# Image 1's pipeline fill rearranged: TensorE transposes, GpSimd adds of squares, cluster sums in one piece

## What is computed

```python
xn = x / jnp.maximum(jnp.linalg.norm(x, axis=1, keepdims=True), EPS)
cn = centroids / jnp.maximum(jnp.linalg.norm(centroids, axis=1, keepdims=True), EPS)
sim = jnp.einsum('bchw,nc->bnhw', xn, cn)
idx = jnp.argmax(sim, axis=1)
onehot = jax.nn.one_hot(idx, N, dtype=x.dtype)
sum_x = jnp.einsum('bhwn,bchw->bnc', onehot, x)
count = jnp.sum(onehot, axis=(1, 2))
centroids_local = sum_x / jnp.maximum(count, 1.0)[..., None]
gathered = centroids_local[jnp.arange(B)[:, None, None], idx]
delta = jnp.transpose(gathered, (0, 3, 1, 2)) - x
alpha = jnp.exp(-jnp.mean(delta * delta, axis=1, keepdims=True))
y = x + alpha * delta
out = jnp.einsum('oc,bchw->bohw', W, y) + b[None, :, None, None]
return jax.nn.relu(out)
```

## Time and profile before

| | us |
|---|---|
| median of 3 runs (414.55 to 415.38) | 415.17 |
| the profiled execution | 415.32 |
| its span in the trace | 413.5 |
| PE busy in the span | 407.3 |
| VectorE, ScalarE, GpSimd busy | 335.2, 255.3, 257.8 |
| first gather matmul of unit 3 / second | 63.68 / 67.30 |

### The profile page before, as it was taken

How to read it: one execution, slowest core, us unless ns; L and a number is a source line. 1 busy time by engine, 2 the same in 40 slices (tenths; PEclk the granted TensorE clock), 3 DMA queues, 4 the chain that set the end, 5 groups by cost and what they waited for, 6 DMA issues and landing times.

```text
span 413.5 us, 5729 instructions
## 1 busy us (share of the span) xinstructions
PE 407.3 (98%) x2064; PEld 287.4 (69%) x2064; DVE 335.2 (81%) x411; ACT 255.3 (62%) x352; POOL 257.8 (62%) x113
## 2 busy tenths in 40 slices
PE   8999999999999999999999999999999999999996
PEld 6744456775877767775867757776777758777885
DVE  2449979789789889899798898898798997898730
ACT  6565564766764775665855666756856657576541
POOL 2000564993699766993979936996769938424420
PEclk9999999999999999999999999999999999999999
DMA  7998496997689395966979575893967240222223
GB/s 261 318 281 160 84 245 171 299 255 150 212 213 297 102 244 161 275 173 170 270 168 250 195 157 190 245 264 115 250 165 220 103 137 3 103 101 103 101 78 126
DMA packets 82047, 76.69 MB, mean 185 GB/s; under 512 B 13844, under 2 KB 56852, under 8 KB 82020
## 3 DMA queue, kind: packets, MB, share of 16 engines
q1 hardware_dynamic: 82020, 76.33, 67.9%
HBM read 48.40 MB, written 25.17 MB: 178 GB/s over the span
## 4 chain that ended last, share of the span: by engine, by line
PE 91%; SPq 5%; DMA 3%; issue 1%; DVE 0%; ACT 0%; DVEq 0%
PE main L922 21%; PE main L923 21%; PE main L924 21%; PE fa L821 8%; PE sump L864 8%; PE gat L898 5%; DMA x<-x 3%; SPq L248 2%; SPq L264 1%; PE al L904 1%; PE fa L830 1%; PE main L966 1%; SPq L242 1%; PE gat L910 1%; PE al L910 1%
## 5 line engine op out<-in xcount | busy, mean ns | idle before, releaser
L922 PE MATMUL main<-yh,wh 128*128 128x512 f32 x376 | 153.5, 408 | 0.0
L923 PE MATMUL main<-yl,wh 128*128 128x512 f32 x376 | 146.7, 390 | 0.0
L924 PE MATMUL main<-yh,wl 128*128 128x512 f32 x376 | 146.6, 390 | 0.0
L331 POOL TENSOR_TENSOR z<-z,x 128x1024 f32<-128x1024 f32 x42 | 99.9, 2399 | 65.1 <-DVE z L458 65.1
L338 POOL TENSOR_TENSOR yl<-z,yh 128x1024 fp32r<-128x1024 f32 x44 | 105.7, 2421 | 54.9 <-ACT yh L616 54.9
L624 ACT ACTIVATE o<-main,bcol 128x512 f32<-128x512 f32 x96 | 65.5, 683 | 59.3 <-PE main L924 59.1
L922 PEld LDWEIGHTS main<-yh,wh 128*128 128x128 f32 x376 | 70.6, 188 | 22.0 <-issue 4.9
L924 PEld LDWEIGHTS main<-yh,wl 128*128 128x128 f32 x376 | 70.6, 188 | 15.2
L923 PEld LDWEIGHTS main<-yl,wh 128*128 128x128 f32 x376 | 70.7, 188 | 13.9
L345 POOL TENSOR_TENSOR xr<-xt 128x2048 f32<-128x2048 f32 x11 | 51.5, 4679 | 18.2 <-DVE xt L371 18.2
L434 DVE TENSOR_TENSOR z<-gat,x 128x1024 f32<-128x1024 f32 x46 | 56.0, 1217 | 6.4 <-PE gat L898 6.1
(11 more groups left out here) (121 smaller groups left out, 367.0 us busy)
## 6 DMA issues: line engine op xcount, KB each, us to landing
out<-o SPq DMA_DIRECT2D x23, 1024.0 KB, 7.3
x<-x SPq DMA_DIRECT2D x21, 1024.0 KB, 6.4
xs<-x SPq DMA_DIRECT2D x84, 256.0 KB, 5.5
x<-x SPq DMA_DIRECT2D x12, 256.0 KB, 5.7
o<-w SPq DMA_DIRECT2D x1, 1024.0 KB, 8.8
out<-o SPq DMA_DIRECT2D x4, 256.0 KB, 2.0
sq<-centroids SPq DMA_DIRECT2D x2, 80.0 KB
oht<-oh SPq DMA_TRANSPOSE x7, 3.7
```

What stands on the lines that cost most here:

```text
L331: pool.tensor_tensor(z, z, X[g // PARTS % 2][:, pair(h), span(g)], ALU.add).then_inc(y_pool, 1)
L922: t_.matmul(main[:, o % 2, :], WH[:, k, rows], YH[g % 2][:, k, :], start=(k == 0), stop=False)
L923: t_.matmul(main[:, o % 2, :], WH[:, k, rows], YL[g % 2][:, k, :], start=False, stop=False)
L924: last = t_.matmul(main[:, o % 2, :], WL[:, k, rows], YH[g % 2][:, k, :], start=False, stop=(k == KC - 1))
```

## The change

Five things are edited, all in the fill.

1. Units 4 and 5 of image 1 (TURNED) are no longer loaded in blocks and transposed by DVE. PE transposes them from X by 32 matmuls against the identity in four groups (`turn`), into the banks `gat` and `main`, and ACT evicts each group (`keep_turned`). Their tokens then lie in plain order (`plain(g)`). `load_xs(4)` and `(5)` go.
2. DIRECT = 3: units 0, 1 and 2 have their four channel blocks of squares added on POOL (`add_chunks`, three 128 x 512 additions a unit) and then summed by one full float32 ones matmul instead of four. Unit 2's squares go to `XR[:, 0]`.
3. The three `sum_clusters(1, .)` stand in one row on PE, in the order 1, 2, 0, and close ahead of the convolution of unit 0.
4. On DVE the argmax of image 1 stands ahead of unit 1's deltas. Unit 3's first transposed half stands ahead of the argmax, its second behind unit 1's deltas. The transposes of unit 6 move ahead of the loop. `y_half(1, 1)` and `low_half(1, 1)` go from POOL to DVE.
5. On SP the x loads of image 1 come first, then `load_xs(3)`, `(6)` and `(7)`, then `transpose_onehot(1)`, then x of units 6 and 7.

Core of the diff:

```diff
-DIRECT = 2
+DIRECT = 3
+
+TURNED = (PARTS + 1, PARTS + 2)
 def y_on_vector(g, h):
-    return g == 0 or (g >= TAIL and h == 1)
+    return g == 0 or (g == 1 or g >= TAIL) and h == 1
 def low_on_vector(g, h):
-    return g >= TAIL and h == 1
+    return (g == 1 or g >= TAIL) and h == 1
+def by_vector(g):
+    return sum(i not in TURNED for i in range(PARTS, g + 1))
+def blocks_loaded(g):
+    return sum(i not in TURNED and (g - i) % 2 == 0 for i in range(PARTS, g + 1))
             def load_xs(g):
-                wait(sp, tr_done, g - 2 - 2)
+                if blocks_loaded(g) > 1:
+                    wait(sp, tr_done, by_vector(g - 2))
...
             load_x(3)
-            load_xs(3)
             load_x(4)
             load_x(5)
-
-            sp.wait_ge(cop_done, 1)
-            load_xs(4)
-            load_xs(5)
+            load_xs(3)
+            load_xs(6)
+            load_xs(7)
             transpose_onehot(1)
-            load_xs(6)
             load_x(6)
-            load_xs(7)
             load_x(7)
             load_xs(8)
...
+            def add_chunks(g):
+                for h in range(2):
+                    sq = squares(g, h)
+                    pool.wait_ge(sq_done, 2 * g + h + 1)
+                    pool.tensor_tensor(sq[:, 0, :], sq[:, 0, :], sq[:, 1, :], ALU.add).then_inc(two_done, 1)
+                pool.wait_ge(two_done, 2 * g + 2)
+                first_two, last_two = squares(g, 0)[:, 0, :], squares(g, 1)[:, 0, :]
+                pool.tensor_tensor(first_two, first_two, last_two, ALU.add).then_inc(four_done, 1)
+
+            add_chunks(0)
+            add_chunks(1)
...
             def sum_squares_direct(g):
-                for k in range(KC):
-                    if k % 2 == 0:
-                        pe.wait_ge(sq_done, 2 * g + k // 2 + 1)
-                    last = t_.matmul(alpha(g), ones[:, :].bitcast(F32), OUT[g][:, k, :],
-                                     start=(k == 0), stop=(k == KC - 1))
-                last.then_inc(one_done, 1)
+                pe.wait_ge(four_done, g + 1)
+                t_.matmul(alpha(g), ones[:, :].bitcast(F32), squares(g, 0)[:, 0, :], start=True, stop=True
+                          ).then_inc(one_done, 1)
...
+            def turn(g, half):
+
+                if g == TURNED[0]:
+                    pe.wait_ge(z_done, 1 + half)
+                else:
+                    pe.wait_ge(xe_act, 6 + half)
+                for t in range(HALF):
+                    at = g % PARTS * UNIT + (HALF * half + t) * P
+                    for k in range(KC):
+                        last = t_.transpose((gat, main)[half][:, t, k * P:(k + 1) * P], X[1][:, k, at:at + P],
+                                            ident[:, :])
                 last.then_inc(xp_done, 1)
```

More of the change, by code:

```diff
@@ L195, in pair, with alpha @@
             return slice(2 * h, 2 * h + 2)
+        def alpha(g):
+            return gat[:, 0, :] if g == 1 else al[:, :]
         def banks(g, h):
-            return main if g < DIRECT and h == 1 else gat
+            return main if g < LAG and h == 1 else gat
         def squares(g, h):
             if g < DIRECT:
-                return OUT[g][:, pair(h), :]
+                return (OUT[0][:, :, :], OUT[1][:, :, :], XR[:, 0, :, :])[g][:, pair(h), :]
             return SQ[:, :, :] if h == 0 else gat[:, :, :]
@@ L353, in _ @@
                 low_half(g, 1)
+                if g == 1:
+                    add_chunks(2)
                 if g + 5 < UNITS and split(g + 5):
@@ L511, in _ @@
             low_weights(3)
[L513 to L517, removed]
+            delta(0, 0)
+            delta(0, 1)
+            transpose_half(3, 0)
             best_sims(1)
             first_best(1)
+            delta(1, 0)
+            delta(1, 1)
+            transpose_half(3, 1)
             scale(0, 0)
@@ L523, in _ @@
             y_half(0, 1)
-            transpose_half(4, 0)
-            transpose_half(4, 1)
+            low_clusters(1)
             scale(1, 0)
             scale(1, 1)
-            transpose_half(5, 0)
-            transpose_half(5, 1)
+            counts(1)
+            y_half(1, 1)
             delta(2, 0)
             delta(2, 1)
-            low_clusters(1)
-            counts(1)
-            add_squares(2)
             rest_of_mean(1)
             parts_of_mean(1)
-            fold(2)
-            low_sum(2)
+            transpose_half(6, 0)
+            low_half(1, 1)
+            transpose_half(6, 1)
             for g in range(PARTS, UNITS):
@@ L588, in keep_transposed, with keep_turned @@
                               ACT.Copy).then_inc(xe_act, 1)
+            def keep_turned(g, half):
+                done = PARTS * 2 + 2 * TURNED.index(g) + half + 1
+                act.wait_ge(xp_done, done)
+                a_.activation(XT[:, g % PARTS, HALF * half:HALF * (half + 1), :], (gat, main)[half][:, :, :],
+                              ACT.Copy).then_inc(xe_act, 1)
             def square(g, h):
                 act.wait_ge(z_done, 2 * g + h + 1)
-                if g < DIRECT:
+                if g < LAG:
                     act.wait_ge(wT_ps, KC)
@@ L631, in copy_sims @@
                 dst, src = simS[:, u, :, :].rearrange("p t s -> p (t s)"), simP[u]
-                if not plain(b):
+                if not plain(g):
                     dst = simS[:, u, :, :].rearrange("p t (q i) -> p q t i", q=Q)
@@ L717, in _ @@
             square(0, 1)
+            keep_turned(4, 0)
+            keep_turned(4, 1)
+            keep_turned(5, 0)
+            keep_turned(5, 1)
+            exp(0)
             square(1, 0)
             square(1, 1)
-            exp(0)
             copy_onehot(1)
+            high_half(0, 0)
+            copy_sums(1)
             exp(1)
-            high_half(0, 0)
             high_half(0, 1)
             count_onehot(1)
-            high_half(1, 0)
+            scale_means(1)
+            high_means(1)
             relu(0, 0)
@@ L737, in _ @@
             relu(0, 3)
-            high_sum(2)
             for g in range(PARTS, UNITS):
@@ L994, in _ @@
             similarities(5)
+            turn(4, 0)
+            transpose_sims(1)
+            turn(4, 1)
+            turn(5, 0)
+            turn(5, 1)
             gather(1, 0)
+            sum_squares_direct(0)
             gather(1, 1)
-            transpose_sims(1)
-            sum_squares_direct(0)
+            sum_clusters(1, 1)
+            sum_clusters(1, 2)
+            sum_clusters(1, 0)
             sum_squares_direct(1)
-            sum_clusters(1, 0)
+            pe.wait_ge(z_done, 4)
             pe.wait_ge(hi_done, 1)
@@ L1004, in _ @@
             high_passes(range(2, KC))
-            sum_clusters(1, 1)
+            gather(2, 0)
+            add_halves(1)
             wait_low(pe, 0, 0)
@@ L1012, in _ @@
                 last.then_inc(main_done, 1)
-            gather(2, 0)
-            sum_clusters(1, 2)
             gather(2, 1)
-            convolve(0, 2, range(0, 2))
-            add_halves(1)
-            convolve(0, 2, range(2, KC))
+            convolve(0, 2)
             convolve(0, 3)
```

45 lines of the change are left out of this document (21 added, 24 removed).

## The result

The changed kernel takes 416.72 us in the median of 5 runs (416.04 to 417.57), the kernel before 415.30 (5 runs, 414.55 to 415.38). The ratio is 1.0039 with a 95% interval of 1.0023 to 1.0056: slower by 0.4%, or 1.4 us. The forecast was 416.3, from 413.3 to 417.3, slower as the likeliest. The profiled execution, 416.04 us, is the fastest of the five; its span is 414.3 us and 0.8 over that of before.

A forecast was written before the change was run, and what follows sets the result against it. PE bounds the kernel, busy 407.3 of 413.5 us, so a shift of unit 3's second gather moves the end. One-hot landing plus 4.4 gives 58.3, plus 10.2 gives 68.5, +1.2: 416.3 us, range 413.3 to 417.3.

The forecast's parts named there:

- The DMA queue: On SP's queue: the transposing one-hot DMA, issued at 46.4, waits behind load_xs(7) and lands at 53.9, not 50.2.
- L: Moment the one-hot's transposing DMA lands: 53.0 to 54.4, taken as 53.9 us.
- rival 2: Same chain, but landing by most DMA engines only, 52.6 to 53.4: 415.0 to 415.8, no change; chance 0.25.
- main case: One-hot waits behind xs7 and lands from 53.4 to 54.6: 415.8 to 417.1 us; chance 0.45.
- The wait at the second gather of unit 2: PE, ready at 55.35, stalls 3 us for VectorE's delta(2,0), done L + 4.4 = 58.3.
- the mark: Start of unit 3's second gather on PE, 67.30 us before; forecast 10.2 after 58.3, at 68.5, +1.2.
- PE's own work: PE in the fill: ones matmuls -4.6, transposes +3.7, stalls -0.4 and -0.8, sum -2.1 us; about -1.7 after ScalarE waits.
- signs of being wrong: One-hot landing within 4.5 us, PE waiting for GpSimd at a ones matmul, clock under 1.00 near 40 us, idle PE after 68.
- rival 3: GpSimd's 128x512 add costs a whole 2.76 us, holding PE 2 us at the ones matmul: 418.3; chance 0.07.
- half price: GpSimd's 128x512 adds cost half its 128x1024 operations, 1.2 to 1.4 us each; 0 to +1.5 kept for it.
- Rival 1: One-hot does not wait for xs7, lands at 50.2; unit 3's second gather at 65.5, time 413.4; chance 0.2.
- Rival 4: PE clock falls to 1.2 GHz behind the four turns, up to 6 us more work, time 419; chance 0.03.

The follow-up runs named there:

- kernel with twice the traffic ahead: Changed kernel with x of unit 6 also issued ahead of transpose_onehot(1) on SP; 420.64 us, ratio to before 1.0119.
- one-hot-first kernel: Changed kernel with transpose_onehot(1) issued ahead of load_xs(7) on SP; 414.42 us, ratio to before 0.9982.

## Why the prediction was right, step by step

- **The bound.** Right: PE is busy 312.00 of 312 us from 68 to 380, and what was lost ahead stays lost.
- **The DMA queue.** Right, the step on which the sign hung. L was put at 53.9 and came at 52.95. As it stands that is in rival 2's bracket, 52.6 to 53.4, and not in the main case's from 53.4 on. Of the 0.9, 0.5 is that this execution ran earlier (unit 0's first gather at 31.70 instead of 32.28, so that the DMA was issued at 45.86, not 46.4). The rest would fit a landing nearer the average DMA engine's time than the slowest's, as rival 2 has it; that is not shown. With nothing, half a megabyte, one, and one and x ahead it landed at 48.6, 50.2, 52.95 and 55.5. Where the Trainium skill, DMA: Bandwidth & Descriptors, Queues, rings and completion order, has each DMA engine take its descriptors in ring order, these runs agree, a transposing DMA included (its packets began at 53 us behind those of x, above), which no row of before showed.
- **The wait at the second gather of unit 2.** 3.0 forecast, 2.49 measured. From L to the gather I summed 4.4 us, and it was 5.1. The term that was mis-sized is `y_half(1, 1)`: 1.14 by starts forecast from the operation of unit 0, 1.84 by starts measured (1.92 long). It began at 54.83 while GpSimd was at `y_half(1, 0)`, which the change had put into the same microseconds, and ended 1.1 us behind that one's end at 55.67. Where it met none of GpSimd's work, in the kernel with twice the traffic ahead, it took 1.21.
- **From there to the mark.** 10.2 forecast, 58.03 to 68.30 is 10.27.
- **PE's own work.** Right for the four turns in the 0.93 each, the ones matmuls at 0.86, the wait for unit 5's x that is gone (32.91 directly behind the gather), and that of the means matmuls. Wrong on one: I had unit 1's additions end before PE needs them. They ended at 47.45 against 46.77, PE waited 0.73, and that cost nothing, since PE then stood 2.49 us for the one-hot. A wait for GpSimd at a ones matmul was among my signs of being wrong, there for rival 3; it came, by another cause. PE was ready for the gather at 55.54, as against 55.35: the early execution and this wait cancel.
- **GpSimd's additions.** The half price was right where GpSimd was alone (1.27 to 1.28), and rival 3's 2.76 is out. It was wrong where VectorE had an operation on two SBUF operands at the same time: 2.15 for the third addition of unit 1, 3.54 for a pair of unit 2. I could have read this in the trace of before. The pair of the earlier trace rows, 2.76 each, began at 46.09 while VectorE was at unit 0's y until 46.98. And the 4679 ns of the earlier trace rows, from which I took that time goes with the columns, is a mean of such cases and others: that operation takes 3.60 us at 305.25, alone, one and a half times the 2.4 of one half as wide, and 5.95 at 318.23, where it meets VectorE's `xr<-xr`. The half price held, but these rows did not support it.
- **Rival 1**'s case, no wait behind xs7, is what the one-hot-first kernel made: 414.4, not 413.4. The 1.0 between is about the two waits for GpSimd, 0.7 and 0.6, that I had taken as hidden. With one of them edited away it is 413.7.
- **Rival 4**, the clock behind the transposes, did not come: 1.00 from 33 to 68 us with all four turns in it. The Trainium skill, TensorE: Matmul & The Clock Gate, Part 4: PE-mode transpose, would not count them as PE busy; this trace shows no fall behind them.
- **The number.** 416.3 forecast, 416.72 measured, and near by luck in part: L came 0.95 early and the chain behind it was 0.7 too long, and the two nearly cancel. From the prologue on, the mark moved by 1.6 us in the traces and the time by 1.4 in the medians, where I had 1.2. Of the 0.7 us by which the median lies over the profiled execution, some 0.6 is likely that execution's early prologue, which the 415.32 that I started from did not have. The range of 4 us held both signs, so that the time lies in it says little; it lies in the main case's narrower one, 415.7 to 417.2, too.

## What to carry to other kernels

Do not issue a DMA whose result a row of short operations waits for behind a large load that is needed only 20 us later; in these runs the order of issues on the one queue was the order of service, so count what is still in flight ahead of the small one. When a chain of small steps (here one-hot, counts, delta) shares in-order engines with the work on the critical path, look at what stands behind each of its waits on every engine: freeing VectorE alone only handed the wait to ScalarE. A gain in the bound engine's own work shows only up to the next thing that is late, so test each part of a change with the others' waits out of the way. And before reading a few tenths out of one trace, count from a point ahead of the change: here the prologue alone moved by over 1 us from one execution to the next.

## What the runs showed of the hardware beyond that

- An operation of VectorE on two float32 operands from SBUF and one of GpSimd did not run beside each other: in each of the meetings read from these traces, whichever began second stood until the first was through, and then took a little less than its usual time. Here are GpSimd and VectorE in the changed kernel:

```profile
45.30 2.15 POOL L368 TENSOR_TENSOR o<-o 128x512 f32<-128x512 f32 x1
47.48 5.85 POOL L350 TENSOR_TENSOR yl<-z,yh 128x1024 fp32r<-128x1024 f32 x2
53.29 2.38 POOL L343 TENSOR_TENSOR z<-z,x 128x1024 f32<-128x1024 f32 x1
```

```profile
45.02 1.28 DVE L491 TENSOR_TENSOR z<-z,x 128x1024 f32<-128x1024 f32 x1
47.47 1.23 DVE L491 TENSOR_TENSOR z<-z,x 128x1024 f32<-128x1024 f32 x1
```

  VectorE's first runs to 46.30, and GpSimd's addition, begun at 45.30, ends 1.15 us later, at 47.45; alone it takes 1.27. VectorE's second runs to 48.70, and GpSimd's pair, begun at 47.48, ends 4.63 us later, at 53.33; alone a pair takes 4.8. The other way round, VectorE's `y_half(1, 1)` took 1.92, 2.44 and 2.75 us in three kernels, and each time ended 1.1 us behind the GpSimd operation that it had met (55.67, 52.95 and 54.16). VectorE's operations with an operand in PSUM, as `scale` at 49.28 (2.35 for two, as ever), ran beside GpSimd without a loss. The Trainium skill, GPSIMD Engine Reference, section Specifications, says that GpSimd shares its SBUF interfaces with VectorE and contends with its instructions that have two SBUF inputs; the trace agrees, and shows the price as the rest of the other's instruction. So an operation moved from GpSimd to VectorE to make room, as `y_half(1, 1)` here, gives part of that back where the two engines then meet.
- The issue of a transposing DMA itself took 1.53 to 1.55 us on SP with nothing ahead of it in the queue, 2.08 behind half a megabyte, and 3.65 behind a whole one in 512-byte packets, but 2.44 behind the end of one and a megabyte of x; so it also holds what SP has to issue next.
- Behind a wait of PE of 5.2 us the next 5.9 us of its work took 1.1 us more, with the granted clock at its lower level for some three microseconds of matmuls. With small matmuls in the wait the clock of the whole run was 1.000 in each of five executions.
